# Second attention of a conv and attention hybrid: three key tiles of the softmax sums moved from GpSimd's additions to accumulating transfers

## What is computed

```
t = t + _L1_attn_ref(_ln_t(t), L1_attn_W, L1_attn_b)
t = t + _L1_ffn_ref(_ln_t(t), L1_ffn_gate_weight, L1_ffn_experts)
...
qk = jnp.einsum('bhqd,bhkd->bhqk', q, k)
qe = jnp.einsum('bhqd,qkd->bhqk', q, embeddings)
weights = jax.nn.softmax((qk + qe) / jnp.sqrt(jnp.float32(d_head)), axis=-1)
output = jnp.einsum('bhqk,bhkd->bhqd', weights, v)
```

## Time and profile before

| | |
|---|---|
| median of three runs | 2824.24 us |
| the profiled execution, its own time | 2824.42 us |
| its span, first to last instruction | 2822.6 us |
| mean granted TensorE clock over the span | 0.940 of full speed |
| PE busy with matmuls | 2467.3 us, 87% |
| DVE busy | 1989.9 us, 70% |
| POOL busy | 1967.6 us, 70% |
| ACT busy | 1403.2 us, 50% |
| all DMA traffic | 278.16 MB, mean 99 GB/s |

### The profile page before, as it was taken

The page is one execution under the profiler, slowest core; times in us unless marked ns, Lnnn a source line. Parts: engine busy times, 40 slices in busy tenths (PEclk is TensorE's granted clock), DMA queues, the critical chain, the costliest instruction groups (busy, mean ns, idle before and its releaser), DMA issues. The chain is left out here.

```text
span 2822.6 us, 47289 instructions
## 1 busy us (share of the span) xinstructions
PE 2467.3 (87%) x18516; PEld 822.8 (29%) x18516; DVE 1989.9 (70%) x3075; ACT 1403.2 (50%) x2548; POOL 1967.6 (70%) x763
## 2 busy tenths in 40 slices
PE   7799999999999999968998999999999999660355
PEld 2464222222222222225552222222222222240234
DVE  4475778778778778627886878788787878278234
ACT  3344555555555655623335666666566666450112
POOL 3123888888888888844445888888888888740773
PEclk9899999999999999989999999999999999885657
DMA  4994222232221232029764233222322231170347
GB/s 80 235 239 146 50 50 50 54 80 60 51 52 50 50 80 64 9 101 278 247 228 142 50 92 70 65 49 72 98 58 64 50 85 29 61 224 0 93 129 257
DMA packets 236268, 278.16 MB, mean 99 GB/s; under 512 B 65393, under 2 KB 171377, under 8 KB 232843
## 3 DMA queue, kind: packets, MB, share of 16 engines
q1 hardware_dynamic: 225548, 249.89, 32.6%
q0 software_dynamic: 6144, 16.85, 1.9%
q10 hardware_dynamic: 4352, 8.39, 0.8%
HBM read 165.17 MB, written 110.67 MB: 98 GB/s over the span
## 5 line engine op out<-in xcount | busy, mean ns | idle before, releaser
L854 POOL TENSOR_TENSOR room_af<-room_af 128x2048 f32<-128x2048 f32 x160 | 725.5, 4535 | 164.2 <-ACT room_af L826 150.4
L1225 POOL TENSOR_TENSOR bias<-bias 128x2048 f32<-128x2048 f32 x160 | 724.6, 4529 | 133.2 <-ACT bias L1195 114.4
L826 ACT ACTIVATE room_af<-PS 128x512 f32<-128x512 f32 x1024 | 555.9, 594 | 396.7 <-PE PS L748 396.7
L635 DVE CUSTOM_DVE_ANT_0 PS<-PS,bias 128x1024 f32<-128x1024 f32 x512 | 620.0, 1241 | 163.1 <-PE PS L623 143.1
L1195 ACT ACTIVATE bias<-PS 128x512 f32<-128x512 f32 x1024 | 555.7, 594 | 356.0 <-PE PS L1123 354.6
L1004 DVE TENSOR_REDUCE row_min_kf<-PS 128x1 f32<-128x1024 f32 x512 | 603.7, 1219 | 120.4 <-PE PS L996 115.5
L741 PE MATMUL PS<-QS_af,KS_af 128*128 128x512 f16 x1024 | 334.5, 387 | 14.3 <-PEq L90 4.5
L1118 PE MATMUL PS<-stacks_kf 128*128 128x512 f16 x1024 | 334.9, 387 | 12.6 <-PEq L90 8.5
L774 PE MATMUL PS<-room_af,V_af 128*32 128x512 f32 x2048 | 273.2, 605 | 1.2 <-ACT room_af L826 1.2
L1143 PE MATMUL PS<-bias,V_kf 128*32 128x512 f32 x2048 | 272.7, 605 | 1.2 <-ACT bias L1195 1.2
L748 PE MATMUL PS<-turned_bias,eyes 64*32 64x512 f16 x4096 | 210.6, 388 | 0.0
(11 more groups left out here) (184 smaller groups left out, 2973.4 us busy)
## 6 DMA issues: line engine op xcount, KB each, us to landing
query_key_halves<-bias SPq DMA_DIRECT2D x32, 768.0 KB, 4.0
query_key_halves<-room_af SPq DMA_DIRECT2D x32, 512.0 KB, 4.3
stacks_kf<-query_key_halves SPq DMA_DIRECT2D x64, 256.0 KB, 7.9
KS_af<-query_key_halves SPq DMA_DIRECT2D x48, 256.0 KB, 4.9
QS_af<-query_key_halves SPq DMA_DIRECT2D x48, 256.0 KB, 6.9
lows_kf<-query_key_halves SPq DMA_DIRECT2D x96, 128.0 KB
token_rows<-rows_t SPq DMA_DIRECT2D x16, 514.0 KB, 4.3
FT_t<-token_rows SPq DMA_DIRECT2D x16, 514.0 KB, 5.6
```

The lines of the kernel that those rows point to most:

```text
L635: nc.vector.tensor_tensor_reduce(out=max_ps[n % len(max_ps)], in0=max_ps[n % len(max_ps)], in1=bias_h[:, g * HG + j, z:z + N], scale=-1.0, ...
L826: nc.scalar.activation(prob[:, n % PR, head, :], score_ps[s % 3], ACT.Exp).then_inc(exps, 1)
L854: nc.gpsimd.tensor_tensor(acc[:, u % 2], so_far, prob[:, n % PR], ALU.add).then_inc(acc_ok, 1)
L1225: nc.gpsimd.tensor_tensor(acc[:, u % 2], so_far, prob[:, n % PR], ALU.add).then_inc(acc_ok, 1)
```

## The change

It changes the stage's summing of tiles, and the order of GpSimd's program:

- The ring has six tiles (`PR` = 6), and holds only tiles 1 to 7 of a unit. Tile 0 is written by ACT into a tile of its own, `sums` (two, by parity).
- Tiles 1, 2 and 3 (`MOVED` = 3) are added onto `sums` by accumulating transfers, which GpSimd issues (`move_tile`), each 1 MB from SBUF to SBUF. Each waits for the one before it: in step 1, in step 2 and in step 5.
- Tiles 4 to 7 are summed by three additions on GpSimd, in steps 5, 6 and 7, into one `acc`. A fourth (`add_sums`) joins `acc` and `sums`, in step 1 of the next unit, behind that unit's first transfer.
- PE makes the denominators from the one part `sums`, in step 4 of the next unit (`DEN` = 4). For the last unit it takes four parts instead: `sums`, `acc` and tiles 6 and 7.
- The reciprocals go to steps 5 to 8 (`REC` = 5), and GpSimd finishes unit u-2 in step 2 of unit u (`FIN` = 2, `BACK` = 2), ahead of the second transfer.
- ACT's waits on the ring follow: for tiles 1 to 3 on the transfer, for the others on `acc_ok`; tile 0 waits for the denominators of the unit two before.

```
-PR = 4
-o1, o2 = HG * CH * PR, HG * CH * (PR + 2)
-prob = zf[:, 0:o1].rearrange("p (r j n) -> p r j n", r=PR, j=HG)
-acc = zf[:, o1:o2].rearrange("p (r j n) -> p r j n", r=2, j=HG)
+PR = 6
+o1, o2 = HG * CH * PR, HG * CH * (PR + 1)
+ring = zf[:, 0:o1].rearrange("p (r j n) -> p r j n", r=PR, j=HG)
+acc = zf[:, o1:o2].rearrange("p (j n) -> p j n", j=HG)
+sums = tile("sums", [P, 2, HG, CH], F32)
-ADDS = KTU - 3
+MOVED = 3
+ADDS = KTU - 1 - MOVED
+STEPS = KTU - 1
+def prob(n):
+    u, kt = divmod(n, KTU)
+    return sums[:, u % 2] if kt == 0 else ring[:, (u * STEPS + kt - 1) % PR]
...
-DEN, REC, TAKE, FIN = 1, 2, 0, 5
+DEN, REC, TAKE, FIN, BACK = 4, 5, 0, 2, 2
...
                 for j in range(HG):
                     last = nc.tensor.matmul(out_ps[j * D:(j + 1) * D, :],
                                             V[:, bb % 2, kt, (g * HG + j) * D:(g * HG + j + 1) * D],
-                                            prob[:, n % PR, j, :], start=(kt == 0), stop=(kt == KTU - 1),
+                                            prob(n)[:, j, :], start=(kt == 0), stop=(kt == KTU - 1),
                                             skip_group_check=True)
                 last.then_inc(weighed, 1)
             def denominators(n, u):
                 pe.wait_ge(max_read, n - 1)
-                pe.wait_ge(acc_ok, ADDS * (u + 1))
-                parts = [prob[:, (KTU * u + kt) % PR] for kt in range(ADDS + 1, KTU)] + [acc[:, u % 2]]
+                if u < NU - 1:
+                    pe.wait_ge(acc_ok, ADDS * (u + 1))
+                    parts = [sums[:, u % 2]]
+                else:
+                    pe.wait_ge(moved, 16 * MOVED * (u + 1))
+                    pe.wait_ge(acc_ok, ADDS * u + 1)
+                    parts = [sums[:, u % 2], acc] + [prob(KTU * u + kt) for kt in range(MOVED + 3, KTU)]
                 for i, part_ in enumerate(parts):
                     for j in range(HG):
                         last = nc.tensor.matmul(max_ps[n % 2][j * D:(j + 1) * D, 0:CH], den_w[:], part_[:, j, :],
...
                     take(n // KTU - 1)
                 if s >= NS_:
                     continue
-                if n >= PR and j == 0:
-                    u, kt = divmod(n - PR, KTU)
-                    act.wait_ge(weighed, n - PR + 1)
-                    if kt <= ADDS:
-                        act.wait_ge(acc_ok, ADDS * u + max(kt, 1))
+                u, kt = divmod(n, KTU)
+                if kt == 0 and j == 0 and u >= 2:
+                    act.wait_ge(max_full, job_at[(u - 2, "den")] + 1)
+                if kt >= 1 and j == 0 and u * STEPS + kt - 1 >= PR:
+                    u, kt = divmod(u * STEPS + kt - 1 - PR, STEPS)
+                    act.wait_ge(weighed, KTU * u + kt + 2)
+                    if kt < MOVED:
+                        act.wait_ge(moved, 16 * (MOVED * u + kt + 1))
                     else:
-                        act.wait_ge(max_full, job_at[(u, "den")] + 1)
+                        act.wait_ge(acc_ok, ADDS * u + max(kt - MOVED, 1))
                 act.wait_ge(full, s + 1)
-                nc.scalar.activation(prob[:, n % PR, j, :], score_ps[s % 3], ACT.Exp,
+                nc.scalar.activation(prob(n)[:, j, :], score_ps[s % 3], ACT.Exp,
                                      scale=-1.0 / (W1S * W1S)).then_inc(exps, 1)
         @block.gpsimd
...
                 r = res_[:, bb % 2, g, first:first + CH]
                 nc.gpsimd.tensor_tensor(r, r, oN[:], ALU.add).then_inc(fin, 1)
+            def move_tile(n):
+                u, kt = divmod(n, KTU)
+                pool.wait_ge(exps, HG * (n + 1))
+                if kt == 1:
+                    pool.wait_ge(weighed, KTU * u + 1)
+                if MOVED * u + kt >= 2:
+                    pool.wait_ge(moved, 16 * (MOVED * u + kt - 1))
+                nc.gpsimd.dma_start(sums[:, u % 2].rearrange("p j n -> p (j n)"), prob(n).rearrange("p j n -> p (j n)"),
+                                    accum_op=ALU.add).then_inc(moved, 16)
             def add_tile(n):
                 u, kt = divmod(n, KTU)
-                if kt == 0 or kt > ADDS:
-                    return
+                first = kt == MOVED + 2
+                done = ADDS * u + kt - MOVED - 2
                 pool.wait_ge(exps, HG * (n + 1))
-                if kt == 1 and u >= 2:
-                    pool.wait_ge(max_full, job_at[(u - 2, "den")] + 1)
-                if kt >= 2:
-                    pool.wait_ge(acc_ok, ADDS * u + kt - 1)
-                so_far = prob[:, (n - 1) % PR] if kt == 1 else acc[:, u % 2]
-                nc.gpsimd.tensor_tensor(acc[:, u % 2], so_far, prob[:, n % PR], ALU.add).then_inc(acc_ok, 1)
+                if done >= 1:
+                    pool.wait_ge(acc_ok, done)
+                nc.gpsimd.tensor_tensor(acc, prob(n - 1) if first else acc, prob(n), ALU.add).then_inc(acc_ok, 1)
+            def add_sums(u):
+                pool.wait_ge(moved, 16 * MOVED * (u + 1))
+                pool.wait_ge(acc_ok, ADDS * (u + 1) - 1)
+                nc.gpsimd.tensor_tensor(sums[:, u % 2], sums[:, u % 2], acc, ALU.add).then_inc(acc_ok, 1)
             for n in range(NU * KTU):
-                add_tile(n)
-                if n % KTU == FIN and n >= KTU:
-                    finish(n // KTU - 1)
-            finish(NU - 1)
+                u, kt = divmod(n, KTU)
+                if kt == 1:
+                    move_tile(n)
+                    if u >= 1:
+                        add_sums(u - 1)
+                if kt == FIN:
+                    if u >= BACK:
+                        finish(u - BACK)
+                    move_tile(n)
+                if kt == MOVED + 2:
+                    move_tile(n - 2)
+                if kt == MOVED + 2 or kt > MOVED + 2 and u < NU - 1:
+                    add_tile(n)
+            for u in range(NU - BACK, NU):
+                finish(u)
         @block.vector
         def _(dve):
...
                 nc.vector.tensor_copy(rec[:, u % 2, :], max_ps[n % 2][:, 0:CH]).then_inc(max_read, 1)
             for n in range(NU * KTU + REC + PIECES):
-                u, piece = n // KTU - 1, n % KTU - REC
+                u = n // KTU - 1
                 if u >= 0 and n % KTU == DEN:
                     take_sums(job_at[(u, "den")], u)
+                u, piece = divmod(n - REC, KTU)
+                u -= 1
                 if n < NU * KTU:
                     for u_, m in step_jobs[n]:
                         max_reduce(dve, job_at[(u_, m)], u_, m)
```

More of the change, by code:

```diff
@@ L934, in attention_keys_first @@
                 LOADS = 16 * 14
-                ADDS = KTU - 3
+                MOVED = 3
[4 more added lines that the diff above has]
+                    return sums[:, u % 2] if kt == 0 else ring[:, (u * STEPS + kt - 1) % PR]
                 sems = [ssem(n) for n in ("stk0", "stk1", "v_in0", "v_in1", "x_in0", "x_in1", "out_st0", "out_st1", "m_in0",
                                           "m_in1", "emb_in", "high_in", "fill", "max_full", "max_read", "full", "exps", "weighed",
-                                          "acc_ok", "recd", "taken", "scaled", "fin")]
+                                          "acc_ok", "moved", "recd", "taken", "scaled", "fin")]
                 (stk0, stk1, v_in0, v_in1, x_in0, x_in1, out_st0, out_st1, m_in0, m_in1, emb_in, high_in, fill, max_full, max_read,
-                 full, exps, weighed, acc_ok, recd, taken, scaled, fin) = sems
+                 full, exps, weighed, acc_ok, moved, recd, taken, scaled, fin) = sems
                 stk, v_in, x_in, out_st, m_in = (stk0, stk1), (v_in0, v_in1), (x_in0, x_in1), (out_st0, out_st1), (m_in0, m_in1)
```

## The result

The change makes the kernel slower: 2976.6 us (median of 4) against 2824.8, ratio 1.0543 with a 95% interval of 1.0519 to 1.0568, so 152 us more, where 65 were forecast. The profiled execution took 2977.84 us (span 2976.1).

The account below looks back on a forecast made before the run. PE bounds the kernel before; after the change POOL's unit, 23.75 + L = 31.15 us, was to exceed PE's 27.25. Against 29.04 over 31 units that is +65 us on 2824.42, thus 2890 us; whole range 2795 to 3000.

Parts of the forecast that it names:

- rival 1: Two full reads, POOL bare on transfers 1 and 2 each unit: 33.25 us a unit, 2955 us; chance 0.29.
- PE's saving: Denominators on PE from one part instead of three: 1.79 us saved a unit, 55 us over 31 units.
- The transfer: Landing of a 1 MB accumulating transfer: 2.4 us fixed plus 3.3 us a pass; 7.4 us taken.
- L: Time from POOL's start on an issue to the transfer's landing, taken as 7.4 us, outer bounds 4.0 and 12.6.
- the two ends: Landing of 5.7 us if the destination's read costs nothing, 9.1 us if it costs a second pass.
- The rule of the Trainium skill: An adding DMA moves data at half a copy's rate, two sources sharing one read ring; landing would be 9.1 us.
- The fit of the Trainium skill: GpSimd transfers, plain copies, take 2.0 us plus bytes over 436 KB per us: 4.4 us estimated for 1 MB.
- The bare wait: On POOL, issue 3 waits uncovered for transfer 2 each unit: 31.15 us a unit against 29.04, +65 us.
- Transfer 1, covered up to L = 8.7: On POOL, issue, join, finish and gaps hide transfer 1 for 8.7 us, so issue 2 adds no wait.
- Transfer 3 and the maxima rows: Transfer 3 runs close to the maxima rows; PE's 3.9 us a unit of spare time absorbs it.
- The 13.8 us: PE was read as already waiting 13.8 us in all, in 30 units, for the maxima rows before the change.
- A constant clock: PE was read at full clock mid-stage; the per-unit sum has no term for a lower clock after stops.

Follow-up runs that it names:

- e5: The change with each accumulating transfer cut from 1 MB to 64 KB, waits and order kept; ratio 0.9818 to the kernel before.
- e14: The change with only transfer 2 at its full 1 MB, the other two at 64 KB; ratio 1.0202 to the kernel before.
- e2: The change with the maxima made 12 instead of 10 steps ahead; ratio 1.0444 to the kernel before.
- e16: The kernel before with the maxima made 12 instead of 10 steps ahead; ratio 1.0008 to the kernel before.
- e13: The change with only transfer 1 at its full 1 MB, the other two at 64 KB; ratio 0.9981 to the kernel before.
- e15: The change with only transfer 3 at its full 1 MB, the other two at 64 KB; ratio 0.9872 to the kernel before.
- e9: The kernel before plus one unneeded 1 MB accumulating transfer a unit, ahead of tile 4's addition, over the maxima rows; ratio 1.0331.
- e10: The kernel before plus one unneeded 1 MB accumulating transfer a unit, ahead of tile 2's addition and of the maxima rows; ratio 1.0007.
- e11: The change with one moved tile, two parts summed on PE in step 4, no join, two accumulators, ring of five; ratio 0.9901 to the kernel before.

## Why the prediction was half right

The time lies inside the whole range of 2795 to 3000 us but far from 2890, and nearest to rival 1's 2955. Three things of the prediction held, and two steps failed.

- *PE's saving*, 31 x 1.79 = 55 us: held. e5 gives 52.
- *The transfer*, L = 7.4: held as a number, 7.1. Its make-up was wrong. 64 KB land in 2.4 us, a plain 1 MB in 4.6, an accumulating one in 7.1: by subtraction, an estimate, 2.2 us for a copy's data and 4.7 with the accumulation. So the accumulation counts in full, and I had a copy's pass too dear (3.3); taking the middle of the two ends gave the right L by luck. Whether it is the second read or the addition that costs, no run separates. The rule of the Trainium skill (Collectives: The Full Stack, "The bandwidth ceiling: the fold count and why AG ≠ RS ≠ AR"), half the rate for an add since it reads two sources, agrees with 4.7 against 2.2 us; the page states it of a collective's reduction. The fit of the Trainium skill (DMA: Bandwidth & Descriptors, "Anatomy of one DMA — SWDGE (gpsimd) path"), 4.4 us by my estimate, agrees with the plain copy's 4.6 and not with the accumulating 7.1.
- *The bare wait*, +65 us: the mechanism held. e14, which has that and nothing else at full size, is 56 us over before (1.0202; the forecast is 1.023). That the sizes are so near is in part luck. A unit with an undisturbed landing is 30.1 to 30.2 us and not 31.15, since POOL's own work is 23.5 us and not 24.8, and that alone would be some +34 us; the longer landings of every third unit, which the sum did not have, brought the mean to 30.7.
- *Transfer 1, covered up to L = 8.7*: failed. I set one L for all three. The cover is 8.1 us, and in units with group loads it takes 8 to 14 us from issue 1 to issue 2. In the change POOL stands 1.78 us a unit before issue 2, 55 us in 31 units, for which the sum had nothing. Rival 1 had the wait, and I gave it the second read as its main cause, where it is the loads; its unit of 33.25 us, near the measured 33.6, comes from an L of 9.1 that no undisturbed transfer has.
- *Transfer 3 and the maxima rows, "PE has 3.9 us a unit to absorb"*: failed. In a unit, the rows are needed before PE comes to the denominators, where its spare time is. Late rows thus delay tiles 1 and 2, for which issues 1 and 2 wait, and PE's delay is added to POOL's chain: 1.20 us a unit before issue 1, 37 us in 31 units, in the change, and 0.0 in e2, where the rows are early. The 13.8 us from which I started were a misreading besides (e16).
- *A constant clock*: not in the sum at all. A stop like that before 1963.81 brings PE back at 0.50 of its clock for some 4 us. In the stage PE is busy 933 us in the change and 873 in e5 with the same products (5390 and 5391 records). Not all of these 60 us lengthen the kernel, since POOL is what the next unit waits for in many units.

The two failed steps were costed at nothing. Together with what the three make of each other, they are the change less e14, 3.4 points or 97 us. By the experiments, the loss of 152 is 52 gained, 46 for transfer 1, 109 for transfer 2, 15 for transfer 3, and 34 (give or take some 20) that appear only when all are there. By POOL's own timeline of the change, 31 units are longer than 29.04 us by 34 us for the bare wait, 15 for the lengthening of transfer 2, 55 before issue 2 and 37 before issue 1; the 11 that are left lie at the stage's two ends and behind it. The wait before issue 1 is near the 34 in size, and neither e13 nor e14 has it (e15: 0.2 us a unit). In e2 it is gone although the clock of the stage is still 0.93, so it needs the late rows. How much the clock adds to it, no run tells.

## What to carry to other kernels

A transfer that replaces an engine's work is cheap only if nothing is queued behind its landing and nothing urgent is in flight with it: look up each small, due transfer (here four rows of 1 KB) before placing a large one: e9 and e10 are 3.2% apart for the same bytes. Sum each queue's program with its longest landing, not its median, and check that an engine's slack comes before the wait that it is to absorb. One transfer with 20 us of room (e11) gained 1%; three in a row lost 5%.

## What was not expected of the hardware

- An accumulating 1 MB transfer within SBUF holds the DMA engines at a share of 0.97 (the window 1960 to 1964 us), and what is issued beside it is late: SP's own four issues of rows took 4.32 us instead of 2.42, and 4.11 in e9.
- POOL starts its next operation 0.57 us into an issue of 0.87. Nothing is won by it: the join's row is 4.83 us instead of 4.53, longer by the 0.30 that it overlaps the issue. An issue of a plain copy is 0.55 us.
- Transfer 2's landing is longer in about every third unit, up to 9.2 us for 7.0 (e14 and the change). In all nine such units of e14, and in all eight of the change between units 1 and 30, a 16 KB packet of the instruction queue starts between issue 2 and issue 3; in most of the other units none does. That the one makes the other was not tested.
- In the kernel before, 14 us in which the weight load waited for the maxima rows could be taken away without gain (e16); PE's own matmuls waited 1.1 us.
